# Expert rows fetched by indirect reads and returned by bounded indirect writes, with dense combining

## The chip, the cores and the metric

The kernel runs on one core of a Trainium2 chip. The metric is device time in microseconds, the median of several executions. TensorE is the matrix engine (PE in the rows; PEld is its weight load), VectorE is DVE, ScalarE is ACT, GpSimd is POOL, SyncE is SP. DMAs are issued from the queues of SP, ACT and POOL ("ACTq", "POOLq", "SPq") and run on the same 16 DMA engines. An indirect DMA takes its row numbers from a table in SBUF and is issued by POOL.

## The reference, cut to what matters

Four layers act on 1250 nodes with 512 features; each is a graph convolution and then a feed-forward block. Three of the four blocks are mixtures of experts and are what the change touches:

- Layer 0 (transformer block): 64 experts, hidden width 256, two experts per token, at most 78 tokens per expert.
- Layer 2: 8 experts, hidden width 512, one expert per token, no limit.
- Layer 3 (transformer block): 8 experts, hidden width 256, two per token, at most 250 tokens per expert; where two experts write one token, the later one stays.

For each expert the computation is

```
xi = rows of the normalised x of its tokens
yi = act(xi @ w1[e] + b1[e]) @ w2[e] + b2[e]
out[token] += gate[token, e] * yi
```

with GELU in layers 0 and 3 and ReLU in layer 2. Everything is float32.

## The kernel before, in words

The stages run one after another, each in blocks of per-engine programs that begin and end together. Tokens lie as 10 tiles of 125 rows (`P` = 125, `T` = 10, `N` = 1250, `D` = 512, `C` = 4 chunks of 128 features).

`route` (from line 1090) computes the logits on TensorE (line 1151), softmax, the best one or two experts and a one-hot mask on VectorE, and each token's place within its expert by triangular products on TensorE (lines 1161 and 1162). VectorE makes three tables of them: `put` (where a token's row goes), `get` (where its result lies) and `gate`; TensorE transposes the gates (line 1171) into `gateT`.

`experts` (line 1309) works in units. In layer 0 a unit is two experts of 78 rows each (`R` = 78, 32 units); in layers 2 and 3 it is one pair of 125-row tiles of one expert (layer 3: 8 units; layer 2: 10 units in this run, with loop counts read from `r.tab`). Each unit has two slots `s`. Its engines do this:

- POOL first scatters every token row into a DRAM buffer `buf`, sorted by expert: 20 indirect DMAs (10 in layer 2), line 1413. Then per unit it stores the two result tiles `yb` into DRAM with plain DMAs (line 1421) and waits until they have landed before it lets VectorE write `yb` again (line 1424).
- SP waits for all scatters and then loads the two 78-row or 125-row tiles `xb` of each unit with plain DMAs (line 1404), one unit ahead.
- ACT issues the weight loads (lines 1474, 1476 and 1479 for the biases) into a ring of four groups, up to three groups ahead, and applies the activation (line 1487).
- TensorE transposes the rows of unit u+1 (line 1442), then multiplies unit u by w1 (line 1453) and w2 (line 1462).
- VectorE adds the residual to x (line 1506) once, scales the transposed rows (line 1516; a plain copy in layer 2, line 1512) and copies results from PSUM to `yb` (line 1525).

The rows of an expert that no token fills are zero rows: `buf` is filled with zeros by 40 DMAs at the start, beside the graph build (line 2308).

`combine` (line 1529) adds the bias of the gated experts (TensorE, line 1562; VectorE, line 1569), fetches the result rows of each token tile by indirect reads on POOL into a ring of four tiles (line 1553), and VectorE multiplies them by the gate and adds them to x (line 1574). In layer 3, SP stores each finished tile to the output (line 1544). The graph convolution that follows layers 0 and 2 begins with row statistics of x in `norm_rows` (line 376).

```
run(pool, store)                      # per unit: two plain stores, wait for both
ahead(u + 1, (g + 1) % 2, True)       # run_ahead: rows of the next unit first,
body(i, u, g, g % 2)                  # then the products of this one
```

Of the kernel before, what the change touches and what calls it, by code (L numbers as in the profile page):

```python
# [6 lines left out]
N = 1250  # L7
D = 512
E = 40000
P = 125  # L10
T = N // P
# [1078 lines left out]
def route(nc, k, yT, wr, br, E_, topk, cap, keep_last, r):  # L1090
# [6 lines left out]
    with ExitStack() as ctx:  # L1097
# [20 lines left out]
        spare = sb("spare", [P, 2, T])  # L1118
# [6 lines left out]
        steps, shifted, exps, masks = sem("route_steps"), sem("shifted"), sem("exps"), sem("masks")  # L1125
        pos_done, gates_ready, gT_done, gT_out = sem("pos_done"), sem("gates_ready"), sem("gT_done"), sem("gT_out")
# [9 lines left out]
        with nc.Block() as block:  # L1136
            @block.gpsimd
            def _(pool):
                pool.iota(ioE[:, :], [[1, E_]], base=0, channel_multiplier=0,
                          allow_small_or_imprecise_dtypes=True).then_inc(iotas, 1)  # L1140

                for c in range(topk):
                    pool.iota(spare[:, c, :], [[topk * P, T]], base=c + r.spare0, channel_multiplier=topk,
                              allow_small_or_imprecise_dtypes=True).then_inc(iotas, 1)

            @block.tensor
            def _(pe):
# [19 lines left out]
                mm.then_inc(pos_done, 1)  # L1167
                pe.wait_ge(gates_ready, 1)
# [5 lines left out]
            @block.scalar  # L1174
            def _(act):
                act.wait_ge(shifted, 1)
                act.activation(W[:, :, :], L[:, :, :], ACT.Exp).then_inc(exps, 1)
                act.wait_ge(gT_done, 1)
                for n, (c0, cn) in enumerate(CH):
                    act.activation(r.gateT[:, c0:c0 + cn], ps[0:E_, 5 + n, 0:cn], ACT.Copy).then_inc(gT_out, 1)  # L1180

            @block.vector
            def _(v):
                s = Steps(v, steps)
                v.wait_ge(iotas, 1 + topk)
# [35 lines left out]
                if cap is None:  # L1221
# [16 lines left out]
                    s.did(v.tensor_copy(r.tab[:, 1, :], blk[0:1, 2, :]))  # L1238
                    s.did(v.tensor_scalar(blk[:, 1, :], blk[:, 2, :], float(2 * P), None, ALU.mult))
# [5 lines left out]
                for c in range(topk):  # L1245
# [3 lines left out]
                    s.wait()  # L1249
                if cap is None:  # L1250
                    s.did(v.tensor_copy(r.put[:, 0, :], pk[:, 0, :]))
                    s.did(v.tensor_copy(r.get[:, 0, :], pk[:, 0, :]))
                    s.did(v.tensor_copy(r.gate[:, 0, :], top[:, :, 0]))
                    s.wait()
                else:
                    for c in range(2):
                        s.did(v.tensor_scalar(keep[:, c, :], pk[:, c, :], float(cap), None, ALU.is_lt))
                        s.did(v.tensor_scalar(tmp[:, c, :], pk[:, c, :], float(cap - 1), None, ALU.min))
                    s.wait()
                    for c in range(2):  # L1260

                        s.did(v.scalar_tensor_tensor(tmp[:, 2 + c, :], ix[:, c, :], float(cap), tmp[:, c, :],
                                                     ALU.mult, ALU.add))
                    s.wait()
                    for c in range(2):
                        s.did(v.tensor_copy(r.get[:, c, :], tmp[:, 2 + c, :]))
                        s.did(v.tensor_tensor(tmp[:, c, :], tmp[:, 2 + c, :], spare[:, c, :], ALU.subtract))
                    s.wait()
                    for c in range(2):
                        s.did(v.tensor_tensor(tmp[:, c, :], tmp[:, c, :], keep[:, c, :], ALU.mult))  # L1270
                    s.wait()
                    for c in range(2):
                        s.did(v.tensor_tensor(r.put[:, c, :], tmp[:, c, :], spare[:, c, :], ALU.add))
# [35 lines left out]
def experts(nc, k, r, rows_in, E_, F, R, tiles, func, w1, b1, w2, affine, buf, ybuf, dynamic, room=None, residual=None):  # L1309
# [7 lines left out]
    FC = F // 128  # L1317
    EPG = 2 if tiles == 1 else 1
    RING = 4
    ROUNDS = E_ // (RING * EPG)  # L1320
    with ExitStack() as ctx:
# [6 lines left out]
        if room is None:  # L1328
            w1s = sb("w1s", [128, RING * EPG, C, F])
        else:  # L1330
            w1s = room(128, (RING * EPG * C, F)).rearrange("p (e c) f -> p e c f", c=C)
        w2s = sb("w2s", [128, RING * EPG, FC, D])
        b1s = sb("b1s", [128, RING * EPG, FC])
        xb = sb("xb", [R, 2, D])
        xbT = sb("xbT", [128, 2, 2, C, R])
        hT = sb("hT", [128, 2, FC, R])
        yb = sb("yb", [R, 2, D])
        put_done = k.gpsimd_dma_semaphore(nc, "put_done")
        stored = [k.gpsimd_dma_semaphore(nc, "stored") for _ in range(2)]
        w_in, w_used = [sem(f"w_in{g}") for g in range(RING)], [sem(f"w_used{g}") for g in range(RING)]  # L1340
        rows_loaded, turned = [sem("rows0"), sem("rows1")], [sem("turned0"), sem("turned1")]
        xT_out, h_done, h_out = [[sem(n + "0"), sem(n + "1")] for n in ("xT_out", "h_done", "h_out")]
        yb_free = [sem("yb_free0"), sem("yb_free1")]
        y_done, y_out = [[sem(n + "0"), sem(n + "1")] for n in ("y_done", "y_out")]
        ps = k.ps

# [11 lines left out]
        def run(eng, body, after=None):  # L1358
            with eng.Fori(0, ROUNDS) as i:
                for g in range(RING):  # L1360
                    group(eng, i, g, body)
                    if after is not None:
                        after(g)

        def run_ahead(eng, ahead, body, after=None):
# [4 lines left out]
            if dynamic:  # L1370
                def both(i, u, g):
                    ahead(u, 0, True)
                    body(i, u, g, 0)
                run(eng, both, after)
                return

            def steps(i, g, last):
                u = i * RING + g
                if not last:
                    ahead(u + 1, (g + 1) % 2, True)  # L1380
# [3 lines left out]
            ahead(0, 0, False)  # L1384
# [6 lines left out]
        def rows_of(u, s):  # L1391
            return bass.ds(nc.s_assert_within(u * (2 * R) + s * R, 0, r.rows - R,
                                              skip_runtime_bounds_check_because="the blocks fit the buffer"), R)

# [3 lines left out]
        with nc.Block() as block:  # L1398
            @block.sync
            def _(sp):  # L1400
                def rows(i, u, g):
                    for s in range(2):
                        sp.wait_ge(turned[s], u + 1)
                        sp.dma_start(xb[:, s, :], buf[rows_of(u, s), :]).then_inc(rows_loaded[s], 16)

                sp.wait_ge(put_done, 16 * r.topk * T)
                run(sp, rows)

            @block.gpsimd
            def _(pool):  # L1410
                for c in range(r.topk):
                    for t in range(T):
                        pool.indirect_dma_start(buf, bass.IndirectOffsetOnAxis(ap=r.put[:, c, t:t + 1], axis=0),
                                                rows_in[:, t, :], None).then_inc(put_done, 16)
                pool.sem_inc(yb_free[0], 1)
                pool.sem_inc(yb_free[1], 1)

                def store(i, u, g):
                    for s in range(2):
                        pool.wait_ge(y_out[s], u + 2)  # L1420
                        pool.dma_start(ybuf[rows_of(u, s), :], yb[:, s, :]).then_inc(stored[s], 16)
# [3 lines left out]
                run(pool, store)  # L1425

            @block.tensor
            def _(pe):
# [7 lines left out]
                def turn(u, parity, used):  # L1436
                    for s in range(2):
                        if used:
                            pe.wait_ge(xT_out[s], u + 1)
                        pe.wait_ge(rows_loaded[s], u * 16 + 16)  # L1440
                        for c in range(C):
                            mm = pe.transpose(ps[:, 4 * s, R * c:R * c + R], xb[:, s, 128 * c:128 * c + 128],  # L1442
# [3 lines left out]
                def products(i, u, g, parity):  # L1446
                    pe.wait_ge(w_in[g], (i + 1) * (48 * EPG))
                    for s in range(2):
                        w = g * EPG + second(s)
                        pe.wait_ge(xT_out[s], u + 2)  # L1450
                        for m in range(FC):
                            for c in range(C):
                                mm = pe.matmul(ps[:, 4 * s + 1, R * m:R * m + R],  # L1453
                                               w1s[:, w, c, 128 * m:128 * m + 128],
# [948 lines left out]
```

## Time and profile before

| | us |
|---|---|
| median of 3 runs | 3489.21 (3488.22 to 3499.31) |
| profiled execution | 3493.22 |
| its span, first to last instruction | 3491.5 |
| TensorE busy / VectorE busy / ACT busy / POOL busy | 2712.7 / 1672.9 / 944.3 / 245.7 |
| layer 0: first scatter, first expert product, combine begins | 1327.06, 1378.94, 1670.23 |
| layer 2: the same three | 2340.49, 2381.05, 2564.25 |
| layer 3: the same three | 3303.39, 3356.97, 3438.55 |

How to read the rows: in the timeline a row gives the start in us from the span's beginning, the time to the end of the last of the merged instructions, engine, line, operation, what is written from what, how many, and in brackets the idle time of that engine before them and what ended it ("issue": nothing that the profile shows). In the table by window the columns are: the stretch, its length, busy us and count of PE, PEld, DVE, ACT and POOL, the clock granted to TensorE (1.00 is 2.4 GHz, 0.50 is 1.2 GHz), the mean busy share of the 16 DMA engines and GB/s. In the waits: who waited, for whom, us in total, times, longest. In the DMA table: destination and source, queue, count, size of each, median us from issue to landing (no size for an indirect one).

### The profile page before, as it was taken

The numbers are of one execution on the slowest core, as the hardware profiler recorded it, in microseconds if no ns is written. First come the engines' busy times: TensorE is split into PE (matmuls) and PEld (weight loads), VectorE is DVE, ScalarE is ACT, GpSimd is POOL, SyncE is SP. The second block draws the span as 40 slices with busy tenths as digits, with TensorE's granted clock in tenths as the row PEclk, the third lists the DMA queues.
The fourth block names the chain that finished last, engine by engine and source line by source line (L and its number), as shares of the span: only waits on it lengthen the run. The fifth ranks groups of instructions, "written<-read, shape, count | busy, mean of one in ns | idle before, by whom it ended". The sixth has DMA issues, their size and how long they took to land. (4 is left out here: it accounts for less than half of the span.)

```text
span 3491.5 us, 42084 instructions
## 1 busy us (share of the span) xinstructions
PE 2712.7 (78%) x12559; PEld 1905.1 (55%) x12560; DVE 1672.9 (48%) x3338; ACT 944.3 (27%) x2087; POOL 245.7 (7%) x247
## 2 busy tenths in 40 slices
PE   5888869967999872999488599946868589998554
PEld 3555546446878642666265266645635367775442
DVE  6777742154888532443433632231132378884323
ACT  1222230112777610111111122211111247774100
POOL 0000000000000103111200000010010000000123
PEclk9999989988999875999698799958979789998576
DMA  7000060211000015997323120014341100000354
GB/s 250 24 0 0 0 170 2 57 42 29 18 21 14 16 33 185 305 314 257 99 51 122 38 58 12 1 66 156 107 102 27 52 25 22 21 15 8 84 165 119
DMA packets 133922, 269.43 MB, mean 77 GB/s; under 512 B 44950, under 2 KB 46182, under 8 KB 132539
## 3 DMA queue, kind: packets, MB, share of 16 engines
q10 hardware_dynamic: 53198, 116.25, 11.2%
q1 hardware_dynamic: 51245, 106.69, 10.0%
q0 software_dynamic: 29376, 45.16, 4.3%
q8 instruction: 59, 0.97, 0.1%
q14 instruction: 44, 0.36, 0.0%
HBM read 189.78 MB, written 73.05 MB: 75 GB/s over the span
## 5 line engine op out<-in xcount | busy, mean ns | idle before, releaser
L1042 DVE TENSOR_REDUCE mx<-ps 125x1 f32<-125x500 f32 (+1 forms) x480 | 274.3, 589 | 57.6 <-PE ps L812 41.0
L243 PE MATMUL ps<-onehot_src,onehot_dst 125*128 x1200 | 258.7, 354 | 42.2 <-DVE onehot_dst L219 17.5
L937 ACT ACTIVATE probs_hi<-ps 125x500 fp32r<-125x500 f32 (+1 forms) x480 | 255.4, 532 | 125.5 <-DVE probs_lo L994 81.1
L218 DVE TENSOR_SCALAR onehot_src<-iota,src_f 125x1250 f16 x400 | 217.6, 544 | 112.4 <-PE ps L243 100.0
L939 ACT ACTIVATE x<-ps 125x500 f32<-125x500 f32 (+1 forms) x480 | 258.7, 539 | 0.0
L994 DVE TENSOR_TENSOR probs_lo<-x,probs_hi 125x1250 fp32r<-125x1250 f32 x160 | 240.9, 1506 | 34.9 <-ACT x L939 31.4
L1525 DVE COPY yb<-ps 78x512 f32<-78x512 f32 (+1 forms) x100 | 68.7, 688 | 349.4 <-PE ps L1462 220.9
L1462 PE MATMUL ps<-w2s,hT 128*78 128x512 f32 (+1 forms) x480 | 217.1, 599 | 2.7 <-ACT hT L1487 2.6
L243 PEld LDWEIGHTS ps<-onehot_src,onehot_dst 125*128 x1200 | 120.8, 102 | 173.6 <-issue 119.7
L1487 ACT ACTIVATE hT<-ps,b1s 128x78 f32<-128x78 f32 (+1 forms) x240 | 66.6, 342 | 519.7 <-PE ps L1453 495.9
L812 PE MATMUL ps<-K_hi_lo,Q_hi_twice 128*125 128x500 f32 (+1 forms) x480 | 182.5, 386 | 22.2 <-DVE mx L1042 16.9
L1442 PE MATMUL ps<-ident,xb 78*128 78x78 f32 (+1 forms) x400 | 51.3, 267 | 183.2 <-DMA xb<-buf 155.1
L820 PE MATMUL ps<-Q_hi_twice,K_hi_lo 128*125 128x500 f32 (+1 forms) x480 | 179.6, 374 | 17.8 <-ACT Q_lo_max L927 5.1
L821 PE MATMUL ps<-Q_lo_max,K_hi_one 65*125 65x500 f32 (+1 forms) x480 | 176.9, 370 | 0.0
L828 PE MATMUL ps<-probs_hi,V_hi 125*128 125x500 f32 (+1 forms) x480 | 174.2, 363 | 0.0
L416 PE MATMUL ps<-ident,xn 125*128 125x125 f32 x280 | 47.1, 351 | 153.4 <-DVE xn L386 153.4
L829 PE MATMUL ps<-probs_hi,V_lo 125*128 125x500 f32 (+1 forms) x480 | 166.3, 361 | 0.0
L1442 PEld LDWEIGHTS ps<-ident,xb 78*128 78x128 f32 (+1 forms) x400 | 38.4, 148 | 226.4 <-DMA xb<-buf 145.2
L1453 PE MATMUL ps<-xbT,room 128*128 128x78 f32 (+1 forms) x1280 | 159.2, 286 | 0.5 <-issue 0.5
L970 POOL TENSOR_TENSOR room<-room 64x600 f32 (+1 forms) x16 | 32.9, 2056 | 1770.8 <-DMA inv<-sums 1770.8
L1453 PEld LDWEIGHTS ps<-xbT,room 128*128 128x128 f32 x1280 | 156.0, 203 | 2.2 <-issue 2.2
L1634 PE MATMUL ps<-w,xT 128*125 128x512 f32 x320 | 141.7, 604 | 11.1 <-ACT xT L1974 8.9
(346 smaller groups left out, 4869.2 us busy)
## 6 DMA issues: line engine op xcount, KB each, us to landing
room<-in_L_ffn_w_p ACTq DMA_DIRECT2D x72, 512.0 KB, 7.1
w2s<-in_L_ffn_w ACTq DMA_DIRECT2D x72, 512.0 KB, 7.3
buf<-zeros SPq DMA_DIRECT2D x37, 512.0 KB
G<-c_spill ACTq DMA_DIRECT2D x2, 5859.4 KB
xb<-buf SPq DMA_DIRECT2D x64, 156.0 KB
yb<-yb POOLq DMA_DIRECT2D x64, 156.0 KB, 7.0
xb<-buf SPq DMA_DIRECT2D x36, 250.0 KB
tv<-in_L_ffn_tv_W_p SPq DMA_DIRECT2D x2, 4096.0 KB
```

The source lines that it names most:

```text
L218: v.tensor_scalar(ohs[:, slot, :].rearrange("p o n -> p (o n)"), io16[:, 0:N], sF[:, bass.ds(tile, 1)], None, ALU.is_equal)
L243: mm_ = pe.matmul(ps[:, 3 * half + c, 0:cn], ohd[:, slot, :].rearrange("p o n -> p (o n)"), ohs[:, slot, c0:c0 + cn].rearrange("p o n -> p ...
L812: pe.matmul(ps[0:P, SQ + cc % 2, 0:cn], Q1[:, j, P * t:P * t + P], K1[:, j, c0:c0 + cn], start=True, stop=True).then_inc(s_done, 1)
L820: pe.matmul(o, K1[:, j, P * t:P * t + P], Q1[:, j, c0:c0 + cn], start=True, stop=False)
L821: pe.matmul(o, K2[:, j, P * t:P * t + P], Q2[:, j, c0:c0 + cn], start=False, stop=True)\
L828: pe.matmul(ps[:, ACC + n, 0:cn], VH[:, t, :], PH[:, t % 2, c0:c0 + cn], start=(t == 0), stop=False)
L937: act.activation(PH[:, t % 2, c0:c0 + cn], ps[0:P, ST + n, 0:cn], ACT.Exp, scale=SCALE).then_inc(p_hi, 1)
L939: act.activation(PT[:, t % 2, c0:c0 + cn], ps[0:P, ST + n, 0:cn], ACT.Exp, scale=SCALE).then_inc(p_out, 1)
L994: v.tensor_tensor(PL[:, t % 2, :], PT[:, t % 2, :], PH[:, t % 2, :].bitcast(fp32), ALU.subtract)\
L1042: v.tensor_reduce(mx[:, t, n:n + 1], ps[0:P, SQ + cc % 2, 0:cn], AX.X, ALU.max)\
L1453: mm = pe.matmul(ps[:, 4 * s + 1, R * m:R * m + R], w1s[:, w, c, 128 * m:128 * m + 128], xbT[:, s, parity, c, :], start=(c == 0), stop=(c ...
L1462: mm = pe.matmul(ps[0:R, 4 * s + 2, :], hT[:, s, m, :], w2s[:, w, m, :], start=(m == 0), stop=(m == FC - 1))
```

## The change

1. `route` no longer makes `put` and `get`. It makes, for every unit and place, the token that sits there: one-hot tables over places (`rowhot`) and units (`unithot`, times token number + 1) on VectorE, 20 products (10 in layer 2) that sum them into PSUM, and a few small steps that give `take` (token to fetch, 0 for an empty place) and `give` (row to write, a number beyond the last row for an empty place). Beside that, SP copies the normalised rows as they are into `rows_dram`, and ACT issues all biases (one DMA) and the first three weight groups at the beginning of `route`.
2. `experts` has no scatter of tokens and no plain loads on SP. POOL issues, per unit, two indirect reads of `rows_dram` for unit u+2 (u+1 in layer 2), then two indirect writes of unit u into `y_dram` with a bound, then waits until both have landed. In layers 0 and 3 `xb` and `yb` get two buffers. The gated biases of `combine` are now added at the start of this block, and the residual after them.
3. `combine` loads whole result tiles with plain DMAs from SP and ACT, in five pieces, and multiplies and adds. In layers 0 and 2 VectorE also takes the row statistics there, so the following `norm_rows` don't.
4. Of the zero fills, 10 are left (rows of `y_dram`).

```diff
@@ route
+                for c in range(topk):
+                    pool.iota(token1[:, c, :], [[P, T]], base=c * N + 1, channel_multiplier=1,
                               allow_small_or_imprecise_dtypes=True).then_inc(iotas, 1)
...
+            @block.sync
+            def _(sp):
+                for to, what in in_two(rowtiles(r.rows_dram), rows_in):
+                    sp.dma_start(to, what).then_inc(r.rows_out, 16)
+                sp.wait_ge(r.rows_out, 32)
...
+                for n in range(topk * T):
+                    c, t = n // T, n % T
+                    pe.wait_ge(hots, 2 * c + 2)
+                    mm = pe.matmul(ps[0:R, 1, 0:NB], rowhot[:, c, t, :], unithot[:, c, t, :], start=(n == 0),
+                                   stop=(n == topk * T - 1))
+                mm.then_inc(slots_done, 1)
...
+                if early is not None:
+                    early(act)
...
+                def rows_of_slots(c, row):
+                    v.tensor_tensor(rowhot[:, c, :, :], ioR[:, :].unsqueeze(1).broadcast_to([P, T, R]),
+                                    row.unsqueeze(2).broadcast_to([P, T, R]), ALU.is_equal).then_inc(hots, 1)
+                def units_of_slots(c, out, hot, number):
+                    return v.tensor_tensor(out, hot, number.unsqueeze(2).broadcast_to([P, T, hot.shape[2]]), ALU.mult)
...
+                v.wait_ge(slots_done, 1)
+                s.did(v.tensor_copy(slots[0:R, 0, :], ps[0:R, 1, 0:NB]))
...
+                s.did(v.tensor_scalar(r.take[:, :], slots[0:R, 1, :], -1.0, 0.0, ALU.add, ALU.max))
+                s.did(v.scalar_tensor_tensor(r.give[:, :], slots[0:R, 0, :], -1.0, slots[0:R, 2, :], ALU.add, ALU.add))
-                        s.did(v.tensor_copy(r.get[:, c, :], tmp[:, 2 + c, :]))
...
-                        s.did(v.tensor_tensor(r.put[:, c, :], tmp[:, c, :], spare[:, c, :], ALU.add))
@@ experts
+    DEEP = 1 if dynamic else 2
+        xb = sb("xb", [R, DEEP, 2, D])
+        yb = sb("yb", [R, DEEP, 2, D])
-            @block.sync
-                        sp.dma_start(xb[:, s, :], buf[rows_of(u, s), :]).then_inc(rows_loaded[s], 16)
-                for c in range(r.topk):
-                    for t in range(T):
-                        pool.indirect_dma_start(buf, bass.IndirectOffsetOnAxis(ap=r.put[:, c, t:t + 1], axis=0),
-                                                rows_in[:, t, :], None).then_inc(put_done, 16)
+                def gather(u, slot):
+                    for s, rows in enumerate(slots_of(r.take, 0, u)):
+                        pool.indirect_dma_start(xb[:, slot, s, :], None, r.rows_dram,
+                                                bass.IndirectOffsetOnAxis(ap=rows, axis=0))\
+                            .then_inc(rows_loaded[slot][s], 16)
+                def scatter(u, slot):
+                    for s in range(2 if dynamic else 0):
+                        pool.wait_ge(y_out[s], u + 2)
+                    for s, rows in enumerate(slots_of(r.give, 1, u)):
+                        if not dynamic:
+                            pool.wait_ge(y_out[s], u + 2)
+                        pool.indirect_dma_start(y_dram, bass.IndirectOffsetOnAxis(ap=rows, axis=0),
+                                                yb[:, slot, s, :], None, bounds_check=2 * N - 1, oob_is_err=False)\
+                            .then_inc(stored[s], 16)
+                def landed(u):
+                    for s in range(2):
+                        pool.wait_ge(stored[s], u * 16 + 16)
+                        pool.sem_inc(yb_free[s], 1)
+                def emptied(u):
+                    for s in range(2):
+                        pool.wait_ge(turned[s], u + 2)
+                pool.wait_ge(r.rows_out, 32)
+                for s in range(2):
+                    pool.sem_inc(yb_free[s], DEEP)
+                gather(0, 0)
+                if dynamic:
...
+                    with pool.Fori(0, units - 1) as u:
+                        emptied(u)
+                        gather(u + 1, 0)
+                        scatter(u, 0)
+                        landed(u)
+                    scatter(units - 1, 0)
+                    landed(units - 1)
+                else:
+                    gather(1, 1)
+                    for u in range(UNITS):
+                        if u + 2 < UNITS:
+                            emptied(u)
+                            gather(u + 2, u % 2)
+                        scatter(u, u % 2)
+                        landed(u)
@@ experts, TensorE and VectorE
+                for t in range(T):
+                    if t >= 2:
+                        pe.wait_ge(bias_taken, t - 1)
+                    pe.matmul(ps[0:P, BIAS[t % 2], :], r.gateT[:, P * t:P * t + P], b2, start=True, stop=True)\
+                        .then_inc(bias_summed, 1)
...
-                if residual is not None:
-                    x, res = residual
-                    v.tensor_tensor(x[:, :, :], x[:, :, :], res[:, :, :], ALU.add)
+                for t in range(T):
+                    v.wait_ge(bias_summed, t + 1)
+                    v.tensor_tensor(x[:, t, :], x[:, t, :], ps[0:P, BIAS[t % 2], :], ALU.add).then_inc(bias_taken, 1)
+                if res is not None:
+                    v.wait_ge(bias_taken, T)
+                    v.tensor_tensor(x[:, :, :], x[:, :, :], res[:, :, :], ALU.add)
                 run_ahead(v, affine_rows, take)
@@ combine
+            def loads(eng, c):
+                src = rowtiles(y_dram[c * N:c * N + N, :])
+                for h in range(HALVES):
+                    for to, what in in_two(Y[:, c, n * h:n * h + n, :], src[:, n * h:n * h + n, :]):
+                        eng.dma_start(to, what).then_inc(got[h], 16)
...
+                for t in range(T):
+                    v.wait_ge(got[t // n], 32 * K_)
+                    for c in range(K_):
+                        if c:
+                            v.wait_ge(added, t * K_ + c)
+                        v.scalar_tensor_tensor(x[:, t, :], Y[:, c, t, :], r.gate[:, c, t:t + 1], x[:, t, :],
+                                               ALU.mult, ALU.add).then_inc(added, 1)
+                    if out is None and t:
+                        v.wait_ge(added, t * K_)
+                        v.bn_stats(k.stats[:, t - 1, :], x[:, t - 1, :])
```

## Rows read from the trace of the kernel before

**Rows 1.** Page, the whole span.

```profile
span 3491.5 us, 42084 instructions
```

**Rows 2.** Timeline, head of layer 0's expert block, to its first result copies.

```profile
1326.33 5.49 DVE L1506 TENSOR_TENSOR x<-x,res 125x5120 f32<-125x5120 f32 x1 [4.20 <-PEq L1136]
...
1327.06 6.02 POOL L1413 DMA_INDIRECT buf<-yn,put  x1 [48.92 <-issue]
...
1360.27 1.19 POOL L1413 DMA_INDIRECT buf<-yn,put  x1 [0.30 <-issue]
...
1378.94 7.04 PE L1453 MATMUL ps<-xbT,room 128*128 128x78 f32 x32
...
1390.16 0.69 DVE L1525 COPY yb<-ps 78x512 f32<-78x512 f32 x1 [1.03 <-PE ps L1462]
```

**Rows 3.** Timeline, layer 0's combine and the normalising step behind it.

```profile
1670.23 17.39 PE L1562 MATMUL ps<-b2r,gateT 64*125 64x512 f32 x20 [11.05 <-PEq L1398]
...
1708.57 0.75 DVE L1574 SCALAR_TENSOR_TENSOR x<-Y,gate,x 125x512 f32<-125x512 f32 x1 [0.87 <-DMA Y<-yb,get]
...
1716.95 6.03 DVE L376 BATCH_NORM_STATS2 row_stats<-x 125x6 f32<-125x512 f32 x10 [7.63 <-PEq L330]
```

**Rows 4.** Table by window: layer 0's loop, its combine, layer 3's loop.

```profile
1450.00:1500.00 50.00, 44.92 (x266) 29.00 (x265) 19.17 (x54) 8.35 (x24) 5.25 (x10) 1.00 0.96 319
...
1670.00:1710.00 40.00, 17.39 (x20) 6.38 (x20) 21.90 (x30) 0.00 (x0) 24.15 (x20) 0.50 0.47 129
...
3370.00:3400.00 30.00, 25.15 (x127) 17.98 (x127) 12.18 (x30) 3.10 (x10) 3.18 (x6) 0.91 0.67 219
```

**Rows 5.** Waits in layer 0's loop, 1376 to 1661.

```profile
DVE yb L1525 <- POOLq L1424: 127.9, 38, 6.3
```

**Rows 6.** Timeline, layer 2: head, transposes between two units, combine.

```profile
2340.49 1.24 POOL L1413 DMA_INDIRECT buf<-xn,put  x1 [41.65 <-issue]
...
2381.05 8.70 PE L1453 MATMUL ps<-xbT,w1s 128*128 128x125 f32 x64
...
2414.28 1.02 PE L1442 MATMUL ps<-ident,xb 125*128 125x125 f32 x8
...
2564.25 17.39 PE L1562 MATMUL ps<-b2r,gateT 8*125 8x512 f32 x20 [7.27 <-PEq L1398]
```

**Rows 7.** Timeline, layer 3: head, a unit from product to store, combine.

```profile
3303.39 5.96 POOL L1413 DMA_INDIRECT buf<-yn,put  x1 [43.80 <-issue]
...
3356.97 5.27 PE L1453 MATMUL ps<-xbT,room 128*128 128x125 f32 x32
...
3423.66 3.81 PE L1453 MATMUL ps<-xbT,room 128*128 128x125 f32 x32 [0.25 <-issue]
...
3432.29 0.53 POOL L1421 DMA_DIRECT2D yb<-yb  x1 [1.18 <-DVE yb L1525]
...
3438.55 17.39 PE L1562 MATMUL ps<-b2r,gateT 8*125 8x512 f32 x20 [7.65 <-PEq L1398]
```

**Rows 8.** Timeline, layer 0's routing: logits, and a pass over 640 elements.

```profile
1277.77 17.03 PE L1151 MATMUL ps<-wr,xnT 128*125 128x64 f32 x80 [8.28 <-PEq L369]
...
1313.54 0.82 DVE L1246 TENSOR_TENSOR work<-onehot,pos 125x640 f32<-125x640 f32 x1
```

**Rows 9.** Waits in the graph build beside the zero fills, 29 to 90.

```profile
DVE onehot_src L218 <- issue: 6.1, 2, 5.5
```

**Rows 10.** DMA table: plain stores and indirect transfers of POOL.

```profile
yb<-yb POOLq DMA_DIRECT2D x64, 156.0 KB, 7.0
...
buf<-yb POOLq DMA_DIRECT2D x20, 250.0 KB, 2.7
...
yb<-yb POOLq DMA_DIRECT2D x16, 250.0 KB, 4.3
...
buf<-yn,put POOLq DMA_INDIRECT x40, 8.6
```

**Rows 11.** Line 1553, its 20 gathers in layer 0's combine, 1661 to 1710.

```profile
DMA to landing us min/median/max: 5.2/5.5/5.8
```

More of the change, by code:

```diff
@@ L1089, in _, with route @@
                 invert(*last[0])
-def route(nc, k, yT, wr, br, E_, topk, cap, keep_last, r):
+def route(nc, k, yT, wr, br, E_, topk, cap, keep_last, r, rows_in, early=None):
     with ExitStack() as ctx:
@@ L1117, in route @@
         tmp = sb("tmp", [P, 4, T])
-        spare = sb("spare", [P, 2, T])
+        token1 = sb("token1", [P, 2, T])
+        R, NB = r.R, r.units
+        rowhot = sb("rowhot", [P, 2, T, R])
+        unithot = sb("unithot", [P, 2, T, NB])
+        ioR, no_row = sb("iota_r", [P, R]), sb("no_row", [P, NB])
+        slots = sb("slots", [P, 3, NB])
+        if cap is None:
+            ioU = sb("iota_u", [P, NB])
+            ahead = sb("ahead", [P, T, NB])
         ioE = sb("iota_e", [P, E_])
@@ L1371, in both @@
                 def both(i, u, g):
-                    ahead(u, 0, True)
+                    ahead(u, u + 1, 0, True)
                     body(i, u, g, 0)
-                run(eng, both, after)
+                with eng.Fori(0, ROUNDS) as i:
+                    for g in range(RING):
+                        group(eng, i, g, both)
+                        if after is not None:
+                            after(g)
                 return
@@ L1557, in _ @@
-            @block.tensor
-            def _(pe):
-                for t in range(T):
-                    if t >= 8:
-                        pe.wait_ge(taken, t - 7)
-                    pe.matmul(k.ps[0:P, t % 8, :], r.gateT[:, P * t:P * t + P], b2, start=True, stop=True)\
-                        .then_inc(summed, 1)
+            if K_ == 2:
+                @block.scalar
+                def _(act):
+                    loads(act, 1)
             @block.vector
@@ L1767, in transformer @@
                   + ([(br[:, :], row(a[pre + "router_b"]))] if bias else []))
[L1768 to L1769 removed]
         R = 78 if cap == 78 else P
[L1771 to L1773 removed]
+        r = Routing(nc, k, ctx, E_, 2, cap, R, rows_dram)
+        with ExitStack() as c4:
+            wts = ExpertBuffers(nc, k, c4, E_, F, R, 1 if R == cap else 2, a[pre + "w1_p"], a[pre + "b1_p"],
+                                a[pre + "w2"], Room(Gf))
+            route(nc, k, xnT, wr, br[:, :] if bias else None, E_, 2, cap, keep_last, r, yn, wts.issue_first)
+            experts(nc, k, r, wts, func, (g2, b2), y_dram, False, x, b2r[:, :], res)
+        combine(nc, k, r, x, y_dram, out)
 def l1_gnn(nc, k, x, w_dram, b_dram, matrix):
@@ L2054, in l2_ffn @@
                                             (b2r[:, :], a["L2_ffn_b2"])])
-        r = Routing(nc, k, ctx, E_, 1, None)
-        route(nc, k, xT, wr, br[:, :], E_, 1, None, False, r)
-        experts(nc, k, r, xn, E_, F, P, 2, ACT.Relu, a["L2_ffn_w1_p"], a["L2_ffn_b1_p"], a["L2_ffn_W2"], None, buf, ybuf, True)
-        combine(nc, k, r, x, b2r[:, :], ybuf, E_)
+        r = Routing(nc, k, ctx, E_, 1, None, P, rows_dram)
+        with ExitStack() as c4:
+            wts = ExpertBuffers(nc, k, c4, E_, F, P, 2, a["L2_ffn_w1_p"], a["L2_ffn_b1_p"], a["L2_ffn_W2"])
+            route(nc, k, xT, wr, br[:, :], E_, 1, None, False, r, xn, wts.issue_first)
+            experts(nc, k, r, wts, ACT.Relu, None, y_dram, True, x, b2r[:, :])
+        combine(nc, k, r, x, y_dram)
 def l1_ffn(nc, k, a, x):
```

301 lines of the change are left out of this document (160 added, 141 removed).

## The prediction

> **What bounds the kernel now.** The whole-span page can't say what this change is worth: it works in three FFN stages, and each has other limits. So I went from the page's span [rows 1] to the timeline at the start and end of each expert block, then to the table by window, the waits and the DMA table.
>
> The first stage (64 experts, 32 units of two) has three parts. A head: POOL issues 20 scatters from 1327.06, first product at 1378.94 [rows 2], so 51.9 us without a product. A loop: from there to the combine at 1670.23 [rows 3], 291.3 us or 9.1 per unit. It is bound by transfers, TensorE close behind: DMA share 0.96 at 319 GB/s, TensorE at its full clock level (1.00) and busy 44.9 of 50 us [rows 4]. VectorE also waits 127.9 us for the single output buffer [rows 5], but with transfers saturated that is their shadow. A tail: combining, paced by VectorE and POOL's gathers in turn, up to the first normalising step at 1716.95 [rows 3].
>
> The second stage (ten units of two 125-row tiles) is bound by TensorE: head 2340.49 to 2381.05, loop to 2564.25 [rows 6]. The third (8 experts) has its head from 3303.39 to 3356.97, loop to 3438.55, combine to the end [rows 7].
>
> **Parts with one answer.** Unseen trifles first. The bias loads that go sat on ACT's queue; the early weights now go out there in the first microseconds of routing, and ACT's Exp is due only after the 17 us of logits [rows 8]: nothing. The copy of the normalised rows to DRAM has all of routing to land: nothing; if that cover went, it is 2.5 MB at 319 GB/s, 8 us per stage. In the graph build 10 of 40 zero fills are left; VectorE sat 6.1 us on "issue" while they ran [rows 9]. Between 0 and -8, I take **-5**.
>
> **Routing gets longer.** Logits show 40 fp32 products (80 pass records) in 17.03 us, 0.43 each; a VectorE pass over 640 elements takes 0.82 [rows 8]. First stage: two unit tables (0.82 each), two row tables (780 elements, 1.0 each), 20 products, of which the second ten end 4.3 us after the first, six small steps, minus some ten removed small ones: about +11. Third stage: row tables of 1250 elements, same 20 products: +12. Second: five passes over 240 elements, one row table, ten products: +10. **+33** in all; ends +22 and +42, since the small steps are estimates.
>
> **The heads shrink, less than the scatters' length.** The expert block now begins with ten bias products on TensorE ahead of the first transposes. In the old combine they took 17.39 us at the half clock level (0.50 granted, TensorE idle before) [rows 3, 4]; it will be idle after routing again. VectorE adds them (0.7 behind), then adds the residual, 5.49 us [rows 2], then scales the first rows; 3 us more until the first product. So product 1 stands 27 us after the block starts (20 in the second stage, which has no residual) and the gathers (issues 1.5 us apart, 1.19 and a gap of 0.30 [rows 2], landing 5.5 [rows 11]) hide under that. The residual add falls on the third pair of gathers and can hold POOL as it held the first scatter, 6.02 us instead of 1.19 [rows 2]; hidden behind the first, half-clock product. Heads: 51.9-27, 40.6-20, 53.6-27 = **-72**.
>
> **The loop of the first stage is the term that decides.** POOL now does everything in one order: gather for u+2 (two issues), scatter u (two issues), wait until both landed, next. Queued behind that wait is the gather for u+3. TensorE must transpose u+2 before it multiplies u+1, so a ring closes over two units: second gather issue +1.5, its landing Lg, 0.5 of transposes (1.02 for eight [rows 6]), 8.63 from the first product to POOL's store issue (3423.66 to 3432.29 [rows 7]), landing Ls. Per unit: (10.6 + Lg + Ls) / 2. POOL alone would allow 4.5 + Ls; that is shorter in nearly all cases. The second output buffer doesn't break the ring.
>
> No row shows a 78-row indirect transfer. A direct one of 250 KB lands in 2.7 alone, an indirect one of 125 rows in 5.5 [rows 10, 11]. Scaled by rows, 78 give 2.7 + 2.8 x 78/125 = 4.45. Alone, then, 2.7 at the least, 5.5 at the most; I take 5.0, between the scaled value and the row nearest in kind. Load adds: a direct store went from 2.7 to 4.3 in the third stage and to 7.0 in the first [rows 10], +1.6 to +4.3. The scatter is issued just when the finished unit's weight slots are refilled (2 MB, 6.6 us at 319 GB/s [rows 4]), so Ls = 5.0 + 3.0 = 8; the gather comes after that burst, Lg = 5. Per unit (10.6 + 13) / 2 = **11.8** against 9.1. The unit's bytes sink (half the places are empty and left out), which would allow less than 9, but nobody waits for bytes then. Loop: first product to its landing 20.6 (slow clock as in 1378.94 to the copy at 1390.16 [rows 2], plus Ls), 31 x 11.8, minus 3 for the last units without gathers, block end 7: 391 against 291, **+99**. Ends: 8.8 per unit (+6) and 13.9 (+164).
>
> **The other loops.** Third stage, 125 rows: Lg 5.5, Ls 5.5 + 1.6, so 11.6 per unit; 17 + 7 x 11.6 - 3 + 4 = 99 against 81.6: **+17**. Second: ten units take 183.2 us [rows 6], 18 each; a gather is issued once the previous scatter has landed, about 8 us after the last copy of its unit, and lands at 15: just hidden. Scatters issued in a pair lengthen the tail by 4.3, stalls under weight loads by 3: **+8**.
>
> **Combining.** 5.1 MB of dense rows at 300 GB/s, 17 us, under 20 steps of 0.78 and ten statistics of 0.6 on VectorE: 22 + 5 until the first piece. Before, 38.3 to the last step at 1708.57 and 6.03 of statistics behind it [rows 3]. First stage **-18**, second (half the rows) **-9**. Third: last piece at about 20, two tiles, last store, with stores sharing the queues 31 instead of 53: **-22**.
>
> **Sum:** -5 + 33 - 72 + 99 + 17 + 8 - 49 = **+31**. The profiled execution took 3493.2 (span 3491.5 [rows 1] and 1.7 around it); its sum is 3524, and the median of the runs lies 4.0 lower: **3520**.
>
> **The rivals.**
> 1. *Short indirect transfers land early* (the other side). Place: the same ring; price 31 us for each microsecond per unit. It breaks even at Lg + Ls = 11 and is measurably faster below 10.3. Half-way between a direct store and the scaled value, 3.6 alone and 5.2 under load, gives (10.6 + 8.8)/2 = 9.7: 3456; with 2.7 and 4.3 it is 8.8: 3427. For it: some 39 of 78 rows are written. Against it: 5.2 is the lowest landing of any of the 20 gathers of the first combine [rows 11]. The Trainium skill (DMA: Bandwidth & Descriptors, "Anatomy of one DMA — SWDGE (gpsimd) path") gives a software-generated transfer about 2.0 us plus its bytes at 436 GB/s, an estimate of 2.4 here, and by that the ring would drop below TensorE's own time, 8.7 per unit, 3424. The direct store's 2.7 agrees, the indirect 5.5 does not [rows 10, 11]. Chance 0.25.
> 2. *Both landings stay loaded*, at the 8.6 that the scatters show as their median [rows 10]: 13.9 per unit, +65: 3585. For it: weights and rows share the queues as in the old head. Against: a slower loop loads them less. Chance 0.15.
> 3. *TensorE's clock falls* to its lower level, since it now idles some 3 us per unit: first products take 7.04 instead of 3.81 [rows 2, 7], half of that per unit, 1.6: 3570. Against: the third stage idles too (25.15 us busy of 30 from 3370) and was granted 0.91 there [rows 4]. Chance 0.08.
> That the bound does not leave empty places out changes 156 KB per unit, half a microsecond of transfer outside the ring; it stays inside the forecast.
>
> **How the numbers follow.** The forecast (11.8 per unit) has 0.52, its own range 3489 to 3551 (10.8 to 12.8 per unit). A measurement of this kernel tells 0.3%, 10.5 us, from no change. Faster by more: rival 1 and a little of the forecast's low end, 0.27. Within: 0.12. Slower: the rest of the forecast and rivals 2 and 3, 0.61. The range takes in most of rivals 1 and 2: 3440 to 3590.
>
> **What would show it.** In the changed profile: first-stage unit near 11.8, TensorE's largest idle time there before the transposes, released by the gather; POOL waiting for its scatter to land; DMA share down to about 0.7; first product 27 us after each block's start, behind ten bias products; route some 10 us longer; combine near 27. Wrong if the unit stays at or below 9, if indirect landings lie under 4.5, or if VectorE or the weights release most of TensorE's idle time.

## The result, and the profile after

The changed kernel takes 3632.73 us (median of 4 runs, 3629.79 to 3634.13) beside 3491.44 for the kernel before in the same comparison: a ratio of 1.040, 95% interval 1.038 to 1.042. Slower, as forecast, but by 141 us where 31 were expected, and outside the range of 3440 to 3590.

The page's first line of the changed kernel, to be held against [rows 1]:

```profile
span 3631.7 us, 41563 instructions
```

Its stages, read off the timelines at the same borders as before (us, change against before; forecast beside it):

| | measured | forecast |
|---|---|---|
| graph build | -4.2 | -5 |
| routing, three stages (7.4, 9.6, 11.3) | +28.3 | +33 |
| heads (-25.2, -20.7, -26.2) | -72.1 | -72 |
| **loop of layer 0** (291.3 to 478.6) | **+187.3** | **+99** |
| loop of layer 2 | +1.3 | +8 |
| loop of layer 3 (81.6 to 106.9) | +25.3 | +17 |
| combining (-14.8, -8.9, -7.8) | -31.5 | -49 |
| between layers 2 and 3 | +5.6 | 0 |
| sum | +140.0 | +31 |

The two spans differ by 140.2; the rest is rounding.

**The head** of layer 0 went as worked out. Timeline of the changed kernel, against [rows 2]:

```profile
1330.27 1.16 POOL L1516 DMA_INDIRECT xb<-rows,take  x1 [56.05 <-SPq L1502]
...
1330.51 17.40 PE L1573 MATMUL ps<-b2r,gateT 64*125 64x512 f32 x20 [2.87 <-issue]
...
1348.67 5.49 DVE L1662 TENSOR_TENSOR x<-x,res 125x5120 f32<-125x5120 f32 x1
1349.96 5.03 POOL L1516 DMA_INDIRECT xb<-rows,take  x1 [14.74 <-PE ps L1582]
...
1356.92 7.04 PE L1593 MATMUL ps<-xbT,room 128*128 128x78 f32 x32
```

The bias products, then the residual, then the first product 26.7 us after the start (27 were forecast). The third gather is held for 5.03 us beside the residual add, where its later ones take 0.97.

**The loop** is where the time went. Two units of it, in the timeline:

```profile
1440.78 0.97 POOL L1516 DMA_INDIRECT xb<-rows,take  x1 [0.30 <-issue]
...
1449.10 0.75 PE L1582 MATMUL ps<-ident,xb 78*128 78x78 f32 x4 [0.93 <-DMA xb<-rows,take]
1449.64 7.04 PE L1593 MATMUL ps<-xbT,room 128*128 128x78 f32 x32
...
1462.50 3.74 PE L1593 MATMUL ps<-xbT,room 128*128 128x78 f32 x32
...
1463.16 0.96 POOL L1526 DMA_INDIRECT expert_rows<-yb,give  x1 [0.74 <-issue]
...
1469.92 0.34 ACTq L1407 DMA_DIRECT2D room<-in_L_ffn_w_p  x1
...
1471.24 0.98 POOL L1516 DMA_INDIRECT xb<-rows,take  x1 [7.12 <-DMA expert_rows<-yb,give]
...
1480.36 7.04 PE L1593 MATMUL ps<-xbT,room 128*128 128x78 f32 x32
```

Read as a ring: a gather is issued at 1440.78 and its rows are used at 1449.10 (8.3 us); the product starts at 1449.64 and its result leaves at 1463.16 (13.5); the next gather waits for that write to land and is issued at 1471.24 (8.1, with the first slot's 1.3 to follow). Then TensorE idles again until those rows land, and the next product starts at 1480.36. The second unit of the pair runs straight behind the first. So the period is one pair: from 1356.92 to 1783.55 fourteen of them, 30.47 us each, or 15.2 per unit, where 11.8 were forecast. The refill of weights (1469.92) goes out just ahead of the gather, not long before it.

In the table by window the transfers are no longer the limit, against [rows 4] (1.00, 0.96 and 319 GB/s in the last three columns):

```profile
1400.00:1450.00 50.00, 30.59 (x154) 21.33 (x155) 12.71 (x36) 4.54 (x13) 13.25 (x14) 0.75 0.60 197
1450.00:1500.00 50.00, 39.97 (x184) 27.80 (x183) 12.62 (x35) 5.63 (x17) 11.66 (x12) 0.73 0.47 152
```

TensorE's groups over the loop (count, busy us and mean ns, then idle before and what ended it), first two of the kernel before, then those of the changed one:

```profile
L1453 PE MATMUL ps<-xbT,room 128*128 128x78 f32 x1024 | 124.7, 282 | 0.3 <-issue 0.3
L1442 PE MATMUL ps<-ident,xb 78*128 78x78 f32 x256 | 28.2, 246 | 70.1 <-DMA xb<-buf 57.5 <-issue 12.6
...
L1593 PE MATMUL ps<-xbT,room 128*128 128x78 f32 x1024 | 169.1, 343 | 0.3 <-issue 0.3
L1602 PE MATMUL ps<-w2s,hT 128*78 128x512 f32 x256 | 139.3, 696 | 0.0
L1582 PE MATMUL ps<-ident,xb 78*128 78x78 f32 x248 | 35.1, 290 | 139.1 <-DMA xb<-rows,take 127.6 <-DVE xbT L1646 6.4 <-issue 5.0
```

Two losses stand there side by side: 127.6 us idle until rows land (57.5 before), and products at a mean of 343 ns (282 before; 275 is the shortest). All fifteen first products behind an idle stretch take 7.04, the second ones 3.74: the lower and the higher of the two clock levels (0.50 granted from 1449.64 to 1456.40, 1.00 from 1462.50 to 1466.00).

**The ends.** Combining in layer 0, then the last layer's to the end of the span:

```profile
1835.56 4.00 SPq L1679 DMA_DIRECT2D Y<-expert_rows  x10
...
1873.53 0.89 DVE L379 BATCH_NORM_AGGREGATE mean_var<-row_stats 125x2 f32<-125x6 f32 x10 [7.99 <-PEq L330]
...
3586.56 4.00 SPq L1679 DMA_DIRECT2D Y<-expert_rows  x10
...
3595.41 25.79 SPq L1687 DMA_DIRECT2D out_x<-x  x10
...
3611.71 2.99 DVE L1702 SCALAR_TENSOR_TENSOR x<-Y,gate,x 125x512 f32<-125x512 f32 x4 [0.43 <-DMA Y<-expert_rows]
```

VectorE is done at 3614.7, but the span lasts to 3631.7; the windows show what runs in that time:

```profile
3585.00:3610.00 25.00, 0.00 (x0) 0.00 (x0) 10.43 (x15) 0.00 (x0) 0.00 (x0) 0.50 0.82 205
3610.00:3632.00 22.00, 0.00 (x0) 0.00 (x0) 4.16 (x6) 0.00 (x0) 0.00 (x0) 0.50 0.30 116
```

Stores alone, at a DMA share of 0.30.

### The profile page after: what moved, and what is told of

Same layout as the page of the kernel before. It is cut to its first block and busy times, and to the rows that moved or that the text cites. A ratio compares the mean times of both kernels' runs of the same rounds, so it can differ in the third digit from the quotient of the medians.

```text
span 3631.7 us, 41563 instructions
## 1 busy us (share of the span) xinstructions
PE 2808.2 (77%) x12659; PEld 1981.1 (55%) x12660; DVE 1685.9 (46%) x3356; ACT 944.7 (26%) x2087; POOL 288.2 (8%) x273
## 5 line engine op out<-in xcount | busy, mean ns | idle before, releaser
L1602 PE MATMUL ps<-w2s,hT 128*78 128x512 f32 (+1 forms) x480 | 238.4, 647 | 0.0
L1593 PE MATMUL ps<-xbT,room 128*128 128x78 f32 (+1 forms) x1280 | 205.6, 337 | 0.5 <-issue 0.5
L1582 PE MATMUL ps<-ident,xb 78*128 78x78 f32 (+1 forms) x400 | 62.6, 307 | 184.0 <-DMA xb<-rows,take 150.8
L1593 PEld LDWEIGHTS ps<-xbT,room 128*128 128x128 f32 x1280 | 202.5, 252 | 2.2 <-issue 2.2
L416 PE MATMUL ps<-ident,xn 125*128 125x125 f32 x280 | 46.5, 346 | 187.3 <-DVE xn L386 187.2
L1582 PEld LDWEIGHTS ps<-ident,xb 78*128 78x128 f32 (+1 forms) x400 | 47.4, 177 | 230.9 <-issue 166.1
L1646 DVE TENSOR_SCALAR xbT<-ps,g,b 128x78 f32<-128x78 f32 (+1 forms) x320 | 93.3, 361 | 149.0 <-PE ps L1582 147.2
```

The costliest lines, as they stand in the source:

```text
L1593: mm = pe.matmul(ps[:, 4 * s + 1, R * m:R * m + R], wts.w1s[:, w, c, 128 * m:128 * m + 128], xbT[:, s, parity, c, :], start=(c == 0), stop ...
L1602: mm = pe.matmul(ps[0:R, 4 * s + 2, :], hT[:, s, m, :], wts.w2s[:, w, m, :], start=(m == 0), stop=(m == FC - 1))
```

## The experiments

Theories: (A) the ring through POOL's order (gather, products, landing of the write) sets the pace; (B) the landings are long because weights stream beside them; (C) the half-level clock after each idle stretch is a term of its own, that adds to A. Rivals: the transfers as such limit; indirect landings are long in themselves; longer products only fill time that would be waited.

**Weights loaded once** (theory B).

```diff
-        for g in range(self.RING - 1):
+        for g in range(self.RING - (self.E_ != 64)):
             self.issue(act, 0, g)
...
                 def weights(i, g):
+                    if wts.E_ == 64:
+                        return
```

> Edit: layer 0 loads the weights of its first four units and never again; the later units compute with those. It leaves out the weight loads of 28 of 32 units (and so computes with other weights), everything else is as it was. Theory (the weight stream is what makes a landing of gather or scatter 8 us where 2 to 3 us are seen without it): the landings fall to 2 to 3.5 us, a pair takes 18 to 22 us, the loop 290 to 350 us, the whole 3440 to 3505 us. Rival (the landings are long by themselves, 78 descriptors of one row each): the loop stays above 430 us and the whole above 3580 us.

Measured: loop from first product to last copy 291.8 us (1362.0 to 1653.8), where by the same borders the changed kernel has 463.5 and the one before 280.3. Whole 3483.00, beside 3497.59 for the kernel before; other weights change the tokens of layer 2 (22 result writes in place of 20), so the loop is the figure to use. Landings over layer 0, of gathers and then of writes:

```profile
DMA to landing us min/median/max: 2.9/3.1/7.2
...
DMA to landing us min/median/max: 2.1/2.5/3.5
```

The changed kernel's own, gathers and writes under weight loads and then the last ones, when no weights are left to load:

```profile
DMA to landing us min/median/max: 3.0/6.0/8.2
...
DMA to landing us min/median/max: 2.9/6.2/7.9
...
DMA to landing us min/median/max: 3.1/3.1/3.5
...
DMA to landing us min/median/max: 2.1/2.5/3.8
```

B holds: the same transfers land in 3.1 and 2.5 without the stream. The Trainium skill (DMA: Bandwidth & Descriptors, "Anatomy of one DMA — SWDGE (gpsimd) path") gives 2.0 us plus bytes at 436 GB/s, an estimate of 2.4 for 156 KB; that agrees with the unloaded writes and not with any landing on the ring. And even so the loop is no shorter than before: at landings of 5.6 together the forecast's formula gives 8.1 per unit, 9.1 were measured (291.8 by 32), against 8.8 before. The clock has a share in that: the first ten units took 10.4 us each, with first products of 5.5 to 7.0 us behind their waits; from 1466.24 to 1639.15 every first product took 3.74 and a unit 8.6. Rival 1 of the prediction asked for 8.8 per unit at landings of 7.0 together; the loop as a whole missed that at shorter ones.

**TensorE kept busy while it waits** (theory C).

```diff
                 def turn(u, nth, parity, used):
+                    if UNITS == 32 and parity:
+                        pe.wait_ge(bias_taken, T)
+                    for _ in range(32 if UNITS == 32 and parity else 0):
+                        pe.matmul(ps[:, 3, 0:128], k.ident[:, :], k.ident[:, :], start=True, stop=True)
```

> Edit: 32 idle 128x128 products into an unused PSUM bank before every second unit's transposes in layer 0, so that TensorE works through the stretch of 9 us in which it waits for the rows; they read only the identity matrix. Theory (the slow products after each idle stretch, 7.0 and 5.1 us in place of 3.7 and 3.6, are a term of their own, 4.9 us per pair of units): the granted clock stays 1.00 through the loop, a pair takes about 26 us in place of 31, the loop about 400 us and the whole about 3555 us. Rival (the ring is set by the transfers alone, and slower products only fill time that would be waited): the products get faster but the pair stays at 30 to 31 us, the whole at 3625 to 3640 us.

Measured: 3593.74, 39 below the changed kernel; about half of what was expected. Its timeline says why:

```profile
1463.80 7.38 PE L1580 MATMUL ps<-ident 128*128 128x128 f32 x64 [0.63 <-issue]
1473.89 3.74 PE L1597 MATMUL ps<-xbT,room 128*128 128x78 f32 x32
...
1489.84 7.41 PE L1580 MATMUL ps<-ident 128*128 128x128 f32 x64
1499.79 6.67 PE L1597 MATMUL ps<-xbT,room 128*128 128x78 f32 x32
...
1529.76 3.74 PE L1597 MATMUL ps<-xbT,room 128*128 128x78 f32 x32
```

In six of the 16 pairs the first product still took 6.2 to 7.0, in the others 3.74. That sorts the pairs of this one execution: from 1473.89 to 1499.79 25.9 us behind a product of 3.74, from there to 1529.76 30.0 behind one of 6.67. Eight pairs of the first kind under weight loads: mean 25.9 (24.7 to 26.4). The six of the second kind: 29.7 (29.0 to 30.6). The two don't overlap, and the idle products are the same in both. The difference lies where the products are: from a pair's first product to its second write 9.1 us at the mean in the eight, 13.4 in the six, 13.6 in the changed kernel; from that write to the next pair's first product 16.8, 16.3 and 16.9. So C holds: the clock costs 3.9 to 4.6 us per pair (against 29.7 and against the changed kernel's 30.47), on the path. Why it still fell in six pairs is open: from the last idle product to the first real one 0.4 to 3.0 us passed in pairs of the first kind, 2.5 to 3.1 in the six.

**Four buffers for the token rows** (theory A).

```diff
-        xb = sb("xb", [R, DEEP, 2, D])
+        XD = 1 if dynamic else 4
+        xb = sb("xb", [R, XD, 2, D])
...
-                    gather(1, 1)
+                    for n in range(1, 4):
+                        gather(n, n)
                     for u in range(UNITS):
-                        if u + 2 < UNITS:
+                        if u + 4 < UNITS:
                             emptied(u)
-                            gather(u + 2, u % 2)
+                            gather(u + 4, u % 4)
```

> Edit: four buffers of token rows in place of two in the layers with a fixed order, so that a gather is issued four units ahead; the wait for each scatter's landing stays where it is. Theory (the ring is gather landing + products + scatter landing over two units): the ring closes over four units, the gather's landing is hidden, and POOL's own turn (issue 2.5 to 4 us and one scatter's landing of 6 to 8 us) is what is left: 9.5 to 12 us per unit, the loop 305 to 385 us and the whole 3460 to 3540 us. Rival (only the scatter's landing counts, since POOL stands there whatever the buffers): the loop stays above 430 us, the whole above 3585 us.

Measured: 3423.34 (before, on the same chip: 3497.59). Loop to the last copy 274.6, 8.6 per unit: shorter than expected (the writes land in 3.9 at the median, where 6 to 8 were put in), and shorter than the 280.3 of before. In layer 3 the same stretch falls from 96.2 to 66.6 (74.0 before). One window and TensorE's groups:

```profile
1450.00:1500.00 50.00, 46.57 (x289) 31.30 (x288) 21.59 (x60) 9.01 (x26) 23.60 (x26) 1.00 0.89 305
...
L1595 PE MATMUL ps<-xbT,room 128*128 128x78 f32 x1024 | 124.9, 282 | 0.3 <-issue 0.3
L1604 PE MATMUL ps<-w2s,hT 128*78 128x512 f32 x256 | 117.7, 603 | 1.5 <-ACT hT L1623 1.5
L1584 PE MATMUL ps<-ident,xb 78*128 78x78 f32 x248 | 24.4, 240 | 23.2 <-issue 11.2 <-DVE xbT L1648 6.4 <-DMA xb<-rows,take 5.5
```

The wait for rows goes from 127.6 to 5.5 us, and with it the products at the lower level: the three groups together are 267.0 us of TensorE, 343.5 in the changed kernel. Nothing was done to the clock; the idle stretches that preceded its falls are gone.

**The landing waited for one unit later** (theory A by the other end of the ring).

```diff
                         scatter(u, u % 2)
-                        landed(u)
+                        if u:
+                            landed(u - 1)
+                    landed(UNITS - 1)
```

> Edit: in the layers with a fixed order of units, POOL waits for the landing of unit u-1's scatter after it has issued unit u's, in place of waiting for unit u's own at once (one completion semaphore per buffer). Theory (POOL's order puts the scatter's landing in the ring: gather landing 8.3 + products + scatter landing 8.1 make 31 us for two units): the next gather no longer waits for the landing of the scatter before it, two landings overlap, a unit takes 10 to 12 us in place of 15.0, the layer-0 loop falls from 479 to 320 to 385 us and the whole to 3475 to 3540 us. Rival (the transfers themselves limit: so many descriptors or so much data per unit): the landings get longer by what they overlap, and the loop stays above 440 us, the whole above 3590 us.

Measured: 3504.66 (before: 3497.59); loop 348.8, 10.9 per unit, inside what A expected. The gathers land in 6.7 at the median and 7.6 at most, no longer than on the ring of the changed kernel (7.2 to 8.2 for the second gather of each pair), so overlapping landings cost little. The clock is still down, for idle time is left (30.0 us of waits for rows):

```profile
1500.00:1550.00 50.00, 44.83 (x208) 30.78 (x208) 14.39 (x40) 7.09 (x22) 15.53 (x16) 0.78 0.63 206
```

**Both, and what then limits.**

> Edit: both of the earlier ones together: four buffers of token rows, and POOL waits for a scatter's landing one unit later. Theory (with four buffers the layer-0 loop at 8.6 us per unit is set by the transfers, 305 GB/s and DMA 0.90, beside which before had 319 GB/s and 0.96, and not by POOL's waits any more): deferring the scatter's landing adds under 10 us in layer 0, the whole 3405 to 3425 us. Rival (POOL's wait for the landing is still in the ring): the loop falls by 20 us or more, the whole under 3400 us.

> Edit: four buffers of token rows, and layer 0 loads the weights of its first four units only; it leaves out the weight loads of the other 28 units and computes them with the first ones. Theory (with four buffers TensorE and the weight stream are close together: 8.6 us per unit against 8.3 us of TensorE's work): the loop falls by 5 to 15 us only, to 260 to 270 us, the whole 3400 to 3420 us. Rival (the weight stream alone is what keeps the four-buffer loop at 8.6 us): the loop falls by more than 30 us, the whole under 3390 us.

Measured: both together 3413.30, loop 268.2 (274.6 with the buffers alone), inside what was expected: the landing of the writes is all but out of the ring. Four buffers without the weight loads: 268.2 as well, while the whole, 3433.33, lies outside its expectation (other weights send other tokens to layer 2's experts). Its window:

```profile
1450.00:1500.00 50.00, 47.07 (x289) 31.35 (x288) 21.68 (x61) 7.74 (x25) 23.51 (x25) 1.00 0.17 50
```

TensorE busy 47.07 of 50 at a DMA share of 0.17: behind the ring TensorE is the limit, at 8.4 per unit (the prediction took 8.7 for it). With the weight stream and the later wait the loop is as long, so the stream adds nothing measurable once the ring is open.

**The output stores split** into 120 and 5 rows.

```diff
-                        sp.dma_start(out[P * t:P * t + P, :], x[:, t, :]).then_inc(stored, 16)
-                    sp.wait_ge(stored, 16 * T)
+                        for to, what in in_two(out[P * t:P * t + P, :], x[:, t, :]):
+                            sp.dma_start(to, what).then_inc(stored, 16)
+                    sp.wait_ge(stored, 32 * T)
```

> Edit: four buffers of token rows, and the output stores of the last layer split into 120 and 5 rows as the loads of expert_rows are. Theory (the last layer's combine gained 8 us in place of 22 because the ten stores of 125 rows run at 128 GB/s, DMA 0.33, which are 20 us for 2.56 MB, and nothing paces them any more): stores of 120 rows run at 200 GB/s or more, the stretch from the first load's issue to the end falls from 44 us to 30 to 36 us, the whole by 8 to 14 us against the four buffers alone, to 3410 to 3416 us. Rival (the stores wait for the additions, or the loads of expert_rows slow by as much as the stores gain): under 3 us.

Measured: 3418.02 (3402.37 to 3433.78), a ratio to before of 0.979, interval 0.975 to 0.983. That is just above the 3410 to 3416 expected, and the runs spread too far to tell 10 us in the whole. One reason is the loop of layer 0, whose code is that of the four buffers alone: it took 287.1 us in this execution, 274.6 in the other. The stretch itself tells the gain. From the first load's issue to the end 31.4 us (3384.54 to 3415.9), 44.1 with four buffers alone. Timeline row and windows:

```profile
3393.45 18.79 SPq L1690 DMA_DIRECT2D out_x<-x  x20
...
3383.00:3408.00 25.00, 0.00 (x0) 0.00 (x0) 11.26 (x16) 0.00 (x0) 0.00 (x0) 0.50 0.88 242
3408.00:3416.00 8.00, 0.00 (x0) 0.00 (x0) 3.33 (x5) 0.00 (x0) 0.00 (x0) 0.50 0.59 203
```

The tail of stores at 116 GB/s is gone. The Trainium skill (DMA: Bandwidth & Descriptors, "Why a DMA increments its semaphore by 16 and not by 1") says that a transfer is spread over the largest number of engines, 16 at most, that divides the slowest dimension of both of its sides; by that, an estimate is 5 engines for 125 rows and 15 for 120. The share of 0.30 agrees with 5 of 16.

**All three.**

> Edit: four buffers, the later wait for the scatter's landing and the split output stores together. By the parts: 0 to 10 us below the version without the later wait, 3400 to 3416 us; against the kernel before a ratio of 0.973 to 0.980.

Measured: 3400.46 (3400.17 to 3401.19), ratio to before 0.9739, interval 0.9722 to 0.9755: faster than both kernels, by 90 and by 232 us. Its loop takes 268.1, and its four runs lie within 1.0 us, where those with the split stores but without the later wait lay within 31.4. So in these runs the later wait also takes away a spread that four buffers leave; what causes that spread was not tried.

## Why the prediction was wrong

**Right:** the direction, and the mechanism named as the deciding term: POOL's single order with a wait for its own write, a ring over two units, TensorE idle before the transposes and released by the gather. More buffers at one end (463.5 to 274.6) and a later wait at the other (348.8) each break it. Heads (-72.1 for -72), build and routing came within 5 us in all; the first two combines (-23.7 for -27) within 4. The -4.2 of the graph build says little: in nine executions with the new fills it ended between 1272.0 and 1277.0, beside 1277.8 in the one before.

**Wrong: the size of the first stage's loop, 88 of the 109 us missed.** In its own terms, per pair of units: 23.6 forecast (twice 11.8), 30.47 measured.

- *The product term, 8.63.* It was taken from a row of layer 3 in which TensorE runs at its higher level [rows 7]. But the ring itself makes TensorE idle for 9 us before each pair, and the first product behind that runs at the lower: 13.6 us from product to write at the mean of the fourteen pairs, 5.0 more than forecast. Of these, 4.5 are the clock (9.1 in the pairs with idle products at the higher level). The forecast had this as rival 3, with a chance of 0.08 and a price of 1.6 per unit, as an alternative to the loaded landings. It is no alternative: it follows from the ring, adds to it, and costs 1.9 to 2.3 per unit. Over fourteen pairs that is 54 to 64 us. The row cited against it (0.91 granted in layer 3) came from a stage that idled in pieces of 1.7 us at most.
- *"The gather comes after that burst, Lg = 5."* The second unit of a pair refills its weights just before POOL is released, so the gather on the ring meets that burst: it landed in 7.6 at the mean (7.2 to 8.2), and 8.2 passed from its issue to the product where 5.5 were put in, 2.7 more. The loop's other gathers, released at the other half of the pair, landed in 3.0 to 3.6.
- *The write's landing, Ls = 8,* was 0.7 too long: 7.3 from the write to the next gather. That it came so near is luck in part. Without the stream the transfers landed in 2.5 and 3.1, where 5.0 was put in, and the load added 4 to 4.5, where 3 was put in for the write and nothing for the gather.

Together with 0.2 less for the second issue that makes the 6.9 per pair (30.47 less 23.6), 96 us over the fourteen. The last units, without weight loads, gave about 8 back, and what is left is the 88.

**The third combine, 14 us:** "with stores sharing the queues 31 instead of 53" took the stores at the rate of the loads. They run at 116 to 128 GB/s where they are alone. In the kernel before they were spread over 39.9 us behind the gathers and hidden; once the adding was quick, they were what came last. Split, the stretch is the forecast's 31.

**Layer 3's loop** missed by 8 us. It has the same ring, and four buffers remove it. The clock is down there too (0.84 granted from 3480 to 3576), but its share and that of the landings were not taken apart. **Layer 2's loop** missed by 7 the other way and routing by 5, which hid a part of the other misses; nothing was tried on them.

**The 5.6 us between layers 2 and 3**, forecast as nothing, can be read from the two traces, though no run tested them. In the step behind layer 2 (its first rows on VectorE are at 2596.24 before and 2728.21 now) ACT issues the load of `G` only when SP's loads of `w` and `b` have landed:

```profile
2590.13 0.42 SPq L341 DMA_DIRECT2D w<-in_L_gnn_W  x1
...
2597.26 1.17 ACTq L396 DMA_DIRECT2D G<-c_spill  x2
...
2637.69 2.08 DVE L1798 TENSOR_TENSOR G<-G,ident 125x125 fp32r<-125x125 f32 x10 [21.53 <-DMA G<-c_spill]
...
2728.16 0.40 SPq L341 DMA_DIRECT2D w<-in_L_gnn_W  x1
...
2735.11 1.23 ACTq L396 DMA_DIRECT2D G<-c_spill  x2
...
2775.42 2.08 DVE L1937 TENSOR_TENSOR G<-G,ident 125x125 fp32r<-125x125 f32 x10 [24.16 <-DMA G<-c_spill]
```

Both kernels take 7 us from the first of these loads to that of `G`. Before, the row statistics ran in that time. Now they are made in the combine, so the step begins where they used to end, `G` is issued 6.9 us after that point in place of 1.0, and VectorE, which waits for it, goes on 5.8 later.

## What to carry to other kernels

Before moving transfers onto one queue with waits between them, draw the ring: every landing that stood between two issues counted in full here, and the ring was broken by depth (more input buffers) or by waiting for a write one unit later. A ring that leaves TensorE idle also changes its clock: take the products of a latency-bound loop at the clock they will have behind the wait, in the sum and not beside it. And when a stage gets shorter, look up what its slow part was pacing and hiding.

## What was not expected of the hardware

- The same 78-row indirect transfer landed in 3.1 (read) or 2.5 us (write) at the median with no weights beside it, and in up to 8.2 and 7.9 beside the two megabytes that a unit's weights are.
- A DMA share of 0.30 and 116 GB/s is all that the stores of 125 rows reached with nothing beside them; as 120 and 5 rows they reached 0.59 and 203, and the end was 12.7 us shorter.
- Removing idle time paid twice: four buffers took 122 us of waiting for rows off TensorE and 76 us off its work.
